# Layer 0 of a graph network: another order of VectorE's work within a step

## What is computed

```python
msg_s = (s_n @ Ws_src)[src] + (s_n @ Ws_dst)[dst]         # and msg_v likewise
w1 = rbf @ W_rbf                                           # weights of an edge
m1_s, m1_v = _cg_tp(msg_s, msg_v, y0, y1, w1...)           # first product: dot, cross, scaled copies
a = leaky(m1_s @ W_alpha) ; a = sum(a * alpha_dot, -1)     # 4 logits of an edge
amax = segment_max(a, dst) ; ex = exp(a - amax[dst])
val_s, val_v = m1_s @ Ws_val, m1_v x Wv_val
val_v = val_v * sigmoid(val_s @ Wg) ; val_s = sigmoid(val_s)
m2_s, m2_v = _cg_tp(val_s, val_v, y0, y1, w2...)           # second product
h = m2 @ Ws_vlin, Wv_vlin
agg = segment_sum(alpha * h, dst)                          # alpha = ex / segment_sum(ex)
```

## Time and profile before

| | |
|---|---|
| median of 3 executions | 10883.89 us (10879.81 to 10886.22) |
| the profiled execution, time and span | 10889.87 us, 10887.1 us |
| layer 0, edges (steps) | from 1453 to 5616 us of the span |
| a step there, mean | 9.41 us |
| a step there, most often | 9.2 us |

### The profile page before, as it was taken

The page is one execution under the profiler, slowest core; times in us unless marked ns, Lnnn a source line. Parts: engine busy times, 40 slices in busy tenths (PEclk is TensorE's granted clock), DMA queues, the critical chain, the costliest instruction groups (busy, mean ns, idle before and its releaser), DMA issues. The chain is left out here.

```text
span 10887.1 us, 242413 instructions
## 1 busy us (share of the span) xinstructions
PE 8864.7 (81%) x46500; PEld 6212.8 (57%) x46501; DVE 8658.5 (80%) x31135; ACT 6961.3 (64%) x26255; POOL 6465.1 (59%) x9502
## 2 busy tenths in 40 slices
PE   3570069999999999999997888887888887888887
PEld 1250058888888888888884444445444445444445
DVE  6850069999999999999978999974666666999995
ACT  0020058888888888888875666644777775777774
POOL 0577777777777777777525555531555551555551
PEclk9965589999999999999999999985999998999996
DMA  7433322222222212221123444441333333444443
GB/s 292 44 82 73 71 42 37 36 37 36 37 36 37 36 35 37 36 36 34 20 43 84 90 89 89 89 67 36 58 58 58 58 57 66 90 90 90 90 89 58
DMA packets 1798441, 691.91 MB, mean 64 GB/s; under 512 B 1586190, under 2 KB 1677258, under 8 KB 1798346
## 3 DMA queue, kind: packets, MB, share of 16 engines
q0 software_dynamic: 219136, 411.56, 15.6%
q1 hardware_dynamic: 1572154, 275.26, 15.1%
q10 hardware_dynamic: 7056, 4.02, 0.1%
HBM read 514.24 MB, written 171.77 MB: 63 GB/s over the span
## 5 line engine op out<-in xcount | busy, mean ns | idle before, releaser
L911 POOL DMA_INDIRECT shared<-table,rec x2640 | 2564.6, 971 | 2236.0 <-DMA efr<-rec_dst 786.9
L993 PE MATMUL bank<-tp,oh 128*128 128x480 f32 (+1 forms) x5280 | 2352.4, 541 | 7.2 <-DVE tp L1070 4.2
L945 ACT ACTIVATE tp<-tp,rec 128x64 f32<-128x64 f32 x7920 | 2031.2, 335 | 239.3 <-DVE tp L1041 174.8
L985 PE MATMUL bank<-w_fc,hT 128*128 128x448 f32 x2640 | 1346.2, 592 | 589.2 <-ACT hT L929 573.0
L993 PEld LDWEIGHTS bank<-tp,oh 128*128 128x128 f32 x5280 | 902.0, 191 | 831.9 <-issue 819.4
L782 POOL DMA_INDIRECT rec_dst<-ACC x784 | 811.6, 1035 | 529.7 <-issue 497.3
L1041 DVE TENSOR_TENSOR tp<-bank,shared 128x256 f32<-128x256 f32 x1320 | 560.6, 425 | 653.9 <-PE bank L993 516.6
L1630 ACT ACTIVATE shared<-bank 128x512 f32<-128x512 f32 x1760 | 942.9, 586 | 122.1 <-PE bank L1705 119.3
L1594 POOL DMA_INDIRECT gat<-table,rec x880 | 889.5, 1011 | 220.5 <-issue 202.6
L929 ACT ACTIVATE hT<-bank 128x128 f32<-128x128 f32 x1320 | 366.5, 278 | 989.2 <-PE bank L979 964.3
L1581 POOL DMA_INDIRECT rec_src<-ACC x784 | 841.6, 1074 | 208.0 <-issue 185.4
(11 more groups left out here) (249 smaller groups left out, 21496.4 us busy)
## 6 DMA issues: line engine op xcount, KB each, us to landing
shared<-table,rec POOLq DMA_INDIRECT x2640
rec_dst<-tp SPq DMA_DIRECT2D x44, 900.0 KB, 23.6
ACC<-in_attrs SPq DMA_DIRECT2D x56, 623.0 KB, 5.1
rec_src<-tp SPq DMA_DIRECT2D x44, 730.0 KB, 19.8
efr<-rec_src SPq DMA_DIRECT2D x440, 64.0 KB
efr<-rec_dst SPq DMA_DIRECT2D x440, 64.0 KB
ACC<-in_attrs SPq DMA_DIRECT2D x196, 130.0 KB
rec<-rec_dst SPq DMA_DIRECT2D x1320, 10.0 KB
```

The costliest lines, as they stand in the source:

```text
L911: nc.gpsimd.indirect_dma_start(out=gatx[:, u, g, 0:L.row], out_offset=None, in_=tables[L.n][:, :], in_offset=IOff(ap=rec[:, u, g, L.idx:L. ...
L945: done = nc.scalar.activation(t[:, g, lo:lo + 64], t[:, g, 0:64], ACT.Copy, scale=rec[:, u, g, L.y + k:L.y + k + 1])
L985: nc.tensor.matmul(pW[u % 2][:, 0:448], hT[:, u % 2, :], fc2[:, :], start=True, stop=True)\
L993: done = nc.tensor.matmul(pS[u % 2][:, 0:TW], oh[:, u, g, :], tp[:, u % 2, g, 64:64 + TW], start=g == 0, stop=g == G - 1)
```

## The change

Only the order in which VectorE's `step` calls its helpers changes; the instructions are the same, and the other engines' orders are the same. `cross_minus` gets the wait for `message` that `scalars_weighed` had given it by standing ahead.

```diff
                     def cross_minus(i, u):
                         v = vectors(msg[:, u % 2])
+                        ve.wait_ge(msg_ready.h, msg_ready.done(i, u))
...
                             message(*b)
-                            scalars_weighed(*b)
                         if d:
                             highest(*d)
                         if b:
                             cross_minus(*b)
+                            scalars_weighed(*b)
                         if d:
                             raised(*d, block_d)
+                            drop(*d, block_d)
                         if a:
                             one_hot(*a)
-                        if d:
-                            drop(*d, block_d)
                         if b:
                             weighed_y0(*b)
-                        if d:
-                            held(*d, block_d)
-                        if b:
                             dot_two(*b)
                             cross(*b)
                         if d:
                             distances(*d)
                         if b:
-                            dot_three(*b)
                             cross_weighed(*b)
                         if c:
                             leaky(*c)
+                            gates(*c)
+                        if b:
+                            dot_three(*b)
+                        if c:
+                            attention(*c)
                         if b:
                             dot_weighed(*b)
                         if c:
-                            gates(*c)
-                            attention(*c)
+                            logits(*c)
                         if e:
                             rescaled(*e, block_e)
+                        if d:
+                            held(*d, block_d)
                         if c:
                             gated_cross_minus(*c, 0)
-                            logits(*c)
-                        if d:
-                            weigh(*d)
-                        if e:
-                            keep(*e, block_e)
-                        if c:
                             gated_cross_minus(*c, 1)
...
                             spread(*c)
+                        if d:
+                            weigh(*d)
+                        if e:
+                            keep(*e, block_e)
```

## The result

| | before | after |
|---|---|---|
| median of 20 executions each | 10887.64 us | 10867.75 us |
| ratio (95% interval) | | 0.9982 (0.9975 to 0.9988) |
| layer 0, first to last message | 4131.6 us | 4119.7 us |
| a turn of four steps, mean | 37.66 us | 37.55 us |
| a turn that nothing disturbs | 37.57 us | 37.04 us |

The change gains 19.9 us, 0.18%, where 42 us were forecast. The table's lower rows are worked out from one trace each, from the starts of the messages and from the granted clock. A *turn* is four successive steps, the third of which ends where the hardware loop comes round. A *stretch* is a time in which TensorE's granted clock is 1.2 instead of 2.4 GHz without a break. An undisturbed turn has no stretch in it or in the turn ahead of it; the number given is the median of these turns.

The account below looks back on a forecast made before the run. VectorE's chain was taken to bound layer 0's steps, with TensorE near. The terms summed to -0.38 us for four steps, -42 us over 110 cycles, from 10884 to 10840 us; range 10775 to 10895 us.

Parts of the forecast that it names:

- the three holes: VectorE's idle places: weighed scalars after the message (0.27 us), one-hot matrix (0.22 us), message at the loop's turn (0.98 us).
- caps a large gain, not a small one: TensorE, busy 8.94 us of a mean step of 9.41 us, was said to limit only a large gain.
- weighed scalars' wait: Behind the message: moving the scalars behind the maximum closes their wait, 4 x 0.27 = -1.08 us a cycle.
- one-hot's wait for the sums: Ahead of the one-hot matrix: its wait for TensorE's sums closes, 3 x 0.22 = -0.66 us a cycle.
- drop ahead: Ahead of the one-hot matrix: the drop reads `mnew`, which ended just before, 4 x 0.12 = +0.48 us a cycle.
- +0.40 for contention: Beside GpSimd's first product: three small VectorE instructions instead of two lie in its window, +0.40 us a cycle.
- loop's turn: Where the hardware loop comes round: `hw` and `keep` cover part of the message's delay, -0.40 us a cycle.
- +0.68 for the moved pair: Beside GpSimd's second product: with weighting and adding moved away, other VectorE instructions are held, +0.68 us a cycle.
- +0.20: Behind the distances and attention: fewer instructions between the cross product or logits and their readers, +0.20 us a cycle.
- Contention isn't worse: Rival, chance 0.18: both contention terms vanish between GpSimd's instructions, gain 160 us, 10724 us; with half, 10784 us.
- the slower one: Rival, chance 0.11: `gated_dot_two` waits for GpSimd's second product, 0.2 us a step, 46 us slower, 10930 us.
- Nothing that can be measured: Rival, chance 0.21: the loop gives 0, contention is somewhat higher, the time stays within 20 us of 10884 us.

Follow-up runs that it names:

- e16: The changed kernel with two more 128-column matmuls per step (three in the fourth) between the groups' heads; ratio 0.9937 to before, layer 0 4066.6 us.
- e8: The kernel before with only weighting and adding of sums moved to the end of the step; layer 0 took 4427.3 us, executed once.
- e9: The changed kernel without the heads' matmuls of every second group on TensorE; ratio 1.0164 to before, layer 0 4322.2 us.
- e17: The changed kernel with two more 16-column matmuls per step (three in the fourth) between the groups' heads; ratio 1.0003 to before, layer 0 4134.1 us.

## Why the prediction was right and wrong

**The views that were read.** They were read rightly in kind: VectorE set the step, and its holes could be closed. The failed step is the sentence after the three holes, that TensorE's nearness "caps a large gain, not a small one". TensorE was taken as a busy share at a fixed speed. Nothing in the sum stands for TensorE's clock, though already in before the clock was down five times in layer 0. By e16 this term is 4119.7 - 4066.6 = +53 us, more than the whole forecast. That the time still lies within the forecast's range is luck: the order gained more than was priced, and the clock took most of it back.

**The terms**, for a turn of four steps, from the medians of each instruction's start in the undisturbed steps of both traces:

| term | forecast | measured |
|---|---|---|
| weighed scalars' wait | -1.08 | gone, no gap left |
| one-hot's wait for the sums | -0.66 | gone; but the pair is held instead, +0.26 a step in three of four |
| drop ahead | +0.48 | +0.44: a gap of 0.03 us where 0.04 was said |
| message to first weighed product, all of these | -0.86, with +0.40 for contention | -1.43 |
| first weighed product to end of step | +0.88 (0.68 and 0.20) | +1.30 |
| loop's turn | -0.40 | -0.40 |
| sum | -0.38 | -0.53 |

The first part of the step turned out better than priced. `mnew` fell from 0.30 to 0.15 us and the second cross term from 0.44 to 0.28, and the drop wasn't held (0.16 us, 0.20 in the fourth step). I had put the contention there, and it fell upon the one-hots: what is slow in both traces is what lies beside GpSimd's dot product (L804). The prediction had this product keep its place behind the message; it moved by 0.3 us. In the ordinary steps the second of GpSimd's L801 instructions takes 0.55 us instead of 0.29, and it now starts together with VectorE's two cross terms, which are not slowed. By these times GpSimd was the one that was held, and its dot product came too late for `mnew` and in time for the one-hots.

The second part was worse. The +0.68 for the moved pair came as priced and a little over (+0.84): `rescaled` takes 0.45 us instead of 0.32 and L1895 0.43 instead of 0.36; in the fourth step, where GpSimd comes later, L1904 takes 0.50 instead of 0.35. The +0.20 measured +0.16. The copy `held`, which the prediction put at nothing, takes 0.26 us instead of 0.21 (0.16 in the fourth step), +0.25 a turn. Ordinary steps gained 0.11 us each and the fourth lost 0.21.

So the order alone was worth more than forecast: 0.53 us a turn, 58 us, where 42 were. Another 7 us of e16's 65 are disturbed turns that before has and e16 hasn't. Of these 65 us the clock took back 53.

**The rivals.** "Contention isn't worse" forecast 10724 us, or 10784 us with half of the two terms, a gain of 100 us and more. The order at the full clock gained 66.6 us (e16), which lies between that and the forecast. Contention was indeed less than priced in the first part of the step, and more in the second. The mechanism of the slower one is shown in e8, where the gates aren't moved; in the whole change the wait stayed out. "Nothing that can be measured" is where the time fell, within 20 us of 10884 us; with 20 executions of each kernel the 0.18% is still clear of noise, and the mechanism is one that this rival didn't name.

**What should show.** The signs in layer 0 came as written: no wait of the scalars; the one-hots directly behind the drop; the gap of 0.03 us behind `mnew`; `rescaled` over 0.4 us; `hw` and `keep` unchanged; 0.5 us at 109 turns; no wait for GpSimd but two. One of the signs against the prediction came too: in 58 steps TensorE set the step.

## What to carry to other kernels

Where TensorE is nearly full beside the engine that is sped up (here 95% busy before the change), read its granted clock in windows as short as a step, and set what one late step costs against the gain. A mean turn that doesn't move while the undisturbed turn does is the mark of it. Compare variants by the undisturbed turn and by the number of stretches together, since the mean alone hid nine orders behind one number. If the clock is the limit, wide matmuls where TensorE otherwise pauses or runs narrow ones may be worth more than the next reordering: in layer 0 they gave 53 us, in a kernel whose output isn't the reference's, where the reordering alone had given 12.

## What the runs showed of the hardware

TensorE's clock fell to half within a stream that was busy 97% of the time (3992 of 4132 us), mostly for 3.41 us at a time and at times that are multiples of 3.413 us apart. Behind the fall shown above the next step lost 0.9 us (9.95 instead of 9.09). The Trainium skill, in TensorE: Matmul & The Clock Gate, section Part 1: The HAM clock gate, says that the gate follows how busy TensorE has recently been, and that where the gate's own clock stands against the work is left to chance at a kernel's start. The traces agree that what TensorE does ahead of a fall matters: the same order of VectorE has 1 stretch in e16 and 234 in e9. No run here shows a difference by chance at the start; after's 20 executions all have the same clock within 0.001. The traces show beyond the page that a loop can fall in step with the gate: mean turns of 37.53 to 37.57 us for undisturbed turns of 36.96 to 37.42. They also show that "busy" in the profile's sense isn't enough: e16 and e17, with matmuls of 128 against 16 columns and the same idle, have 1 and 37 stretches.

Where VectorE and GpSimd both read SBUF, either can be the one that is held. In after GpSimd's L801 took 0.55 us instead of 0.29 beside VectorE's cross terms, and in e8 0.91 us beside three VectorE instructions that kept their length; a moment later in after VectorE's one-hots were the slow ones.

A one-hot matrix, which reads one 128-column operand and a scalar from SBUF, took 0.44 and 0.38 us where before it took 0.29 and 0.28, in ordinary steps in which it now lies beside GpSimd's product. The Trainium skill, in SBUF — State Buffer, section Who interferes with whom, lets instructions of this kind contend with GpSimd in their fast modes. The longer times agree with that; in which mode they ran no run here shows. The prediction had taken from this section only that an instruction with at most one SBUF input doesn't contend, without the fast modes, and so had no price for the one-hots.
